# The second q, k, v stage: rows from the matrix engine with the bias in PSUM, turned in fp32, stored in 1 MB pieces

## What is computed

```python
def act_quant(x):                     # per row of 512
    s = 127.0 / clip(max(abs(x)), EPS)
    return clip(round(x * s), -128, 127) / s
def weight_quant(w):                  # -1, 0, 1 times the mean
    s = 1.0 / clip(mean(abs(w)), EPS)
    return clip(round(w * s), -1, 1) / s
def bitlinear(x, w, b):
    return act_quant(x) @ weight_quant(w).T + b
xn  = rmsnorm(x, g1) * (1 + scale) + shift      # scale, shift: one pair of rows per batch
qkv = bitlinear(xn, w_qkv, b_qkv)
q, k, v = split(qkv)                            # attention follows: softmax(q k^T / sqrt(32)) v
```

## Time and profile before

| | |
|---|---|
| median of 3 runs | 4297.87 us (4294.86 to 4299.38) |
| profiled execution | 4297.65 us, its span 4295.9 us, mean granted clock 0.944 |
| busy, share of the span | PE 3864.4 us (90%), DVE 2841.2 (66%), ACT 2651.5 (62%), POOL 850.9 (20%) |
| all DMA | 419.67 MB, mean 98 GB/s |

### The profile page before, as it was taken

One profiled execution on the slowest core, in us unless ns is written; L12 is line 12 of the kernel. 1 busy time (PEld: TensorE's weight loads), 2 busy tenths in 40 slices (PEclk: granted clock), 3 DMA queues, 4 the chain that ended last, 5 costly groups with the idle time before them and its releaser, 6 DMA issues. The chain is left out here.

```text
span 4295.9 us, 69382 instructions
## 1 busy us (share of the span) xinstructions
PE 3864.4 (90%) x26385; PEld 2562.5 (60%) x26436; DVE 2841.2 (66%) x5335; ACT 2651.5 (62%) x4619; POOL 850.9 (20%) x932
## 2 busy tenths in 40 slices
PE   8998999999999554989999945689999999997999
PEld 7875666666666443777788822256666666663444
DVE  3327888888888455333421146678888888886887
ACT  2227888888888222222222224378888888885887
POOL 0015555555555122000000022200000000001221
PEclk9999999999999777999999967789999999998999
DMA  5445332333321455334431044453332223313221
GB/s 184 181 155 130 75 63 58 63 67 71 63 58 28 147 175 175 111 128 140 162 120 49 30 150 176 159 130 62 63 74 63 57 63 67 70 28 128 72 70 42
DMA packets 309208, 419.67 MB, mean 98 GB/s; under 512 B 90959, under 2 KB 167267, under 8 KB 308875
## 3 DMA queue, kind: packets, MB, share of 16 engines
q1 hardware_dynamic: 308878, 415.23, 34.6%
HBM read 257.54 MB, written 157.32 MB: 97 GB/s over the span
## 5 line engine op out<-in xcount | busy, mean ns | idle before, releaser
L555 ACT ACTIVATE Sn<-Sn,mn 128x1024 f32<-128x1024 f32 x1024 | 1175.0, 1147 | 30.6 <-DVE mn L583 18.8
L521 PEld LDWEIGHTS pt<-ident,Sn 128*128 128x128 f32 x8192 | 881.0, 141 | 421.0 <-issue 413.5
L521 PE MATMUL pt<-ident,Sn 128*128 128x128 f32 x8192 | 1123.2, 280 | 1.2 <-DVE PT L547 0.5
L545 ACT ACTIVATE PT<-pt 128x512 f32<-128x512 f32 x1280 | 738.3, 598 | 235.8 <-PE pt L521 235.8
L489 PE MATMUL sp<-KS,QS 97*128 97x512 f32 (+1 forms) x2048 | 733.7, 440 | 40.4 <-DMA KS<-cpad 18.9
L583 DVE CUSTOM_DVE_ANT_0 Sn<-sp,biastile 128x1024 f32<-128x1024 f32 x512 | 624.1, 1219 | 145.2 <-PE sp L489 113.6
L585 DVE TENSOR_SCALAR_CACHE_REDUCE Sn<-sp 128x1024 f32<-128x1024 f32 x512 | 624.0, 1219 | 127.6 <-PE sp L489 127.6
L628 POOL TENSOR_SCALAR biastile<-dist,ascale 128x1024 f32<-128x1024 f32 x512 | 576.0, 1125 | 497.2 <-DVE mn L583 483.5
L510 PE MATMUL po<-PT,Vp 128*32 128x256 f32 x8192 | 651.4, 391 | 0.0
L547 DVE COPY PT<-pt 128x512 f32<-128x512 f32 x768 | 531.0, 691 | 118.9 <-PE pt L521 118.9
L1044 ACT ACTIVATE gf<-pf,b1T 128x512 f32<-128x512 f32 x128 | 88.3, 690 | 562.5 <-PE pf L989 535.9
(11 more groups left out here) (210 smaller groups left out, 4839.9 us busy)
## 6 DMA issues: line engine op xcount, KB each, us to landing
QS<-s_qhi SPq DMA_DIRECT2D x128, 256.0 KB, 5.1
KS<-s_khi SPq DMA_DIRECT2D x128, 256.0 KB, 7.1
KS<-s_klo SPq DMA_DIRECT2D x64, 256.0 KB, 6.1
QS<-s_qlo SPq DMA_DIRECT2D x64, 256.0 KB, 6.9
Vp<-s_v SPq DMA_DIRECT2D x64, 256.0 KB, 7.7
s_o<-og SPq DMA_DIRECT2D x32, 512.0 KB, 8.7
xA<-in_x SPq DMA_DIRECT2D x8, 1024.0 KB, 5.9
s_qhi<-qstage SPq DMA_DIRECT2D x32, 256.0 KB, 2.0
```

What stands on the lines that cost most here:

```text
L521: op = nc.tensor.transpose(ps[:, i, :], sn[:, (g * HALF + i) * P:(g * HALF + i + 1) * P], K.ident[:])
L545: nc.scalar.activation(dst, src, ACT.Copy).then_inc(*s_cp_act.up())
L555: nc.scalar.activation(sn[:], sn[:], ACT.Exp, scale=-1.0, bias=mn[n % 3][:, t:t + 1], accum_out=sums[n % 5][:, t:t + 1]).then_inc(*s_exp.up())
```

## The change

Only stage D changes, and it is the same arithmetic in another order. The quantised tile is the stationary operand for q, k and v alike, so that all three come out as rows (`project`). Each group has a fifth matmul with six rows: six bf16 rows of the bias against six bf16 columns that hold pieces of the inverse scale. So the PSUM tile holds (product + bias / scale), and one multiplication by the scale, a column, ends it: on ACT for q and k (`scale_row`), on DVE for v (`scale_v`). q and k are then turned by PE as fp32 (`turn_row`), and ACT and DVE take the halves out of PSUM (`high_half`, `low_half`; the factor of q is in both). The bias rows are split in three on DVE after the first tile's first operation, and SP places them by three DMAs (`bias_rows`). POOL makes the pieces of the inverse scale (`inverse_pieces`) and the whole inverse root (five small operations, as in stage F); DVE multiplies by G first and by the root with the shift added in one operation. Every engine has a new order. PE works tile by tile, not block by block, in single PSUM tiles (`px`; `pr` for q, k, v; `pT` for q, k). q and k are gathered over four tiles and stored as four DMAs of 1 MB, v as before with four buffers, x with eight. On POOL, iteration s has the scale and the pieces of tile s-2, at each batch's start the product of G, and then the root of tile s.

```diff
+def bias_rows(K, S, name, n, s_raw, s_split, s_row):
+    nc, dve, sp = K.nc, K.dve, K.sp
+    rows, rest = S.sb("brow" + name, [6, n], BF16), S.sb("brest" + name, [6, n])
+    second, third = S.sb("bp2" + name, [6, n], BF16), S.sb("bp3" + name, [6, n], BF16)
+    def load(src):
+        nc.sync.dma_start(rest[:], src.partition_broadcast(6)).then_inc(*s_raw.up(16))
+    def split():
+        dve.wait_ge(s_raw, 16)
+        nc.vector.tensor_copy(rows[:], rest[:]).then_inc(*dve.own.up())
+        dve.settle()
+        nc.vector.tensor_tensor(rest[:], rest[:], rows[:], ALU.subtract).then_inc(*dve.own.up())
+        dve.settle()
+        nc.vector.tensor_copy(second[:], rest[:]).then_inc(*dve.own.up())
+        dve.settle()
+        nc.vector.tensor_tensor(third[:], rest[:], second[:], ALU.subtract).then_inc(*s_split.up())
+    def place():
+        sp.wait_ge(s_split, 1)
+        for row, (_, piece) in enumerate(PIECES):
+            if piece:
+                nc.sync.dma_start(rows[row:row + 1, :], (None, second, third)[piece][row:row + 1, :]).then_inc(*s_row.up(16))
+    return rows, load, split, place
...
+def inverse_pieces(K, rc, left, sc, winv, s_rc):
+    nc, pool = K.nc, K.pool
+    nc.gpsimd.tensor_scalar(left, sc, winv, 1.0, ALU.mult, ALU.mult).then_inc(*pool.own.up())
+    pool.settle()
+    nc.gpsimd.tensor_copy(rc[:, 0:3], left.to_broadcast([P, 3])).then_inc(*pool.own.up())
+    pool.settle()
+    nc.gpsimd.tensor_tensor(left, left, rc[:, 0:1], ALU.subtract).then_inc(*pool.own.up())
+    pool.settle()
+    nc.gpsimd.tensor_copy(rc[:, 3:5], left.to_broadcast([P, 2])).then_inc(*pool.own.up())
+    pool.settle()
+    nc.gpsimd.tensor_tensor(rc[:, 5:6], left, rc[:, 3:4], ALU.subtract).then_inc(*s_rc.up())
...
-        x_l = S.loads("xD", 6, [P, D])
+        x_l = S.loads("xD", 8, [P, D])
...
+        rc, rT = [S.sb(f"rcD{i}", [P, 6], BF16) for i in range(2)], [S.sb(f"rTD{i}", [6, P], BF16) for i in range(2)]
+        sm = [S.sb(f"smD{i}", [P, 16]) for i in range(16)]
+        row = {w: [S.sb(f"{w}rowD{i}", [P, D]) for i in range(2)] for w in "qk"}
+        st = {w: S.stores(w + "stD", 2, [P, 2, DC, BLK], F32R, 2) for w in "qk"}
+        vst = S.stores("vstD", 4, [P, D])
+        px = S.ps("pxD", [P, 2 * D], BF16)
+        pr, pT = {w: S.ps(f"p{w}D", [P, D]) for w in "qkv"}, {w: S.ps(f"pT{w}D", [P, DC, P]) for w in "qk"}
...
+            x, s = x_l.take(sp, i, 1, (s_xg, i + 1), (s_sq, i + 1))
...
-            load_x(0)
             load_b(0)
+            load_bias(a["L1_cond_b_qkv"])
             for i in range(1, 4):
                 load_x(i)
             nc.sync.dma_start(wq[:], K.tern_s["qkv"].rearrange("(c p) n -> p c n", p=P)).then_inc(*s_w.up(16))
+            place_bias()
             for b in range(1, B):
                 load_b(b)
             for s in range(NT + TAIL):
                 if s + 4 < NT:
                     load_x(s + 4)
-                for i, j in groups(s - 1):
-                    if j < 2 * DC:
-                        w, c = "qk"[j // DC], j % DC
-                        buf, sem = qst.of(2 * DC * i + j)
-                        sp.wait_ge(s_qlo, 2 * DC * i + j + 1)
-                        for n, part in enumerate(("hi", "lo")):
-                            nc.sync.dma_start(K.qk_s[w, part][c * P:(c + 1) * P, i * BLK:(i + 1) * BLK],
-                                              buf[:, n, :].bitcast(F32)).then_inc(*sem.up(16))
-                    else:
-                        t = j - 2 * DC
-                        buf, sem = vst.of(TPB * i + t)
-                        sp.wait_ge(s_v, TPB * i + t + 1)
-                        nc.sync.dma_start(K.v_s[i * BLK + t * P:i * BLK + (t + 1) * P, :], buf[:]).then_inc(*sem.up(16))
-            qst.done(sp)
-            vst.done(sp)
-        def turn(i):
-            blk, t = divmod(i, TPB)
-            ps = pt_r.take(pe, i, (s_xT, i + 1))
+                i = s - 4
+                if 0 <= i < NT:
+                    buf, sem = vst.of(i)
+                    sp.wait_ge(s_v, i + 1)
+                    nc.sync.dma_start(K.v_s[i * P:(i + 1) * P, :], buf[:]).then_inc(*sem.up(16))
+                    if i % TPB == TPB - 1:
+                        cols = slice(i // TPB * BLK, (i // TPB + 1) * BLK)
+                        for w in "qk":
+                            buf, sem = st[w].of(i // TPB)
+                            sp.wait_ge(s_lo[w], i + 1)
+                            for n, part in enumerate(("hi", "lo")):
+                                nc.sync.dma_start(K.qk_s[w, part][:, cols].rearrange("(c p) t -> p c t", p=P),
+                                                  buf[:, n].bitcast(F32)).then_inc(*sem.up(16))
+            for r in (vst, st["q"], st["k"]):
+                r.done(sp)
...
+        def turn_x(i):
             pe.wait_ge(s_xq, i + 1)
+            pe.wait_ge(s_rc, i + 1)
+            if i >= 1:
+                pe.wait_ge(s_xT, i)
             for c in range(DC):
...
+                nc.tensor.transpose(px[:, c * P:(c + 1) * P], xq[i % 2][:, c * P:(c + 1) * P], K.identb[:])
+            nc.tensor.transpose(px[0:6, D:D + P], rc[i % 2][:], K.identb[:]).then_inc(*s_Tx.up())
+        def project(i, w):
+            pe.wait_ge(s_xT, i + 1)
+            if i >= 1:
+                pe.wait_ge(s_v if w == "v" else s_e[w], i)
+            cols = slice("qkv".index(w) * D, ("qkv".index(w) + 1) * D)
+            for d in range(DC):
+                nc.tensor.matmul(pr[w][:], xT[i % 2][:, d, :], wq[:, d, cols], start=d == 0, stop=False)
+            nc.tensor.matmul(pr[w][:], rT[i % 2][:], brow[:, cols], start=False, stop=True).then_inc(*s_m[w].up())
+        def turn_row(i, w):
+            pe.wait_ge(s_e[w], i + 1)
+            if i >= 1:
+                pe.wait_ge(s_lo[w], i)
+            for c in range(DC):
+                op = nc.tensor.transpose(pT[w][:, c, :], row[w][i % 2][:, c * P:(c + 1) * P], K.ident[:])
+            op.then_inc(*s_T[w].up())
         def tensor_program():
             pe.wait_ge(s_w, 16)
+            pe.wait_ge(s_row, 48)
             for s in range(NT + TAIL):
...
+                if 0 <= s - 1 < NT:
+                    project(s - 1, "k")
+                    project(s - 1, "v")
+                if s < NT:
+                    turn_x(s)
+                if 0 <= s - 1 < NT:
+                    turn_row(s - 1, "q")
+                    turn_row(s - 1, "k")
+                if s < NT:
+                    project(s, "q")
...
+        def copy_xT(i):
+            act.wait_ge(s_Tx, i + 1)
+            if i >= 2:
+                act.wait_ge(s_m["v"], i - 1)
+            nc.scalar.activation(rT[i % 2][:], px[0:6, D:D + P], ACT.Copy)
+            nc.scalar.activation(xT[i % 2][:], px[:, 0:D].rearrange("p (c q) -> p c q", q=P), ACT.Copy).then_inc(*s_xT.up())
+        def scale_row(i, w):
+            act.wait_ge(s_dq, i + 1)
+            act.wait_ge(s_m[w], i + 1)
+            if i >= 2:
+                act.wait_ge(s_T[w], i - 1)
+            nc.scalar.activation(row[w][i % 2][:], pr[w][:], ACT.Copy, scale=col(i, 9)).then_inc(*s_e[w].up())
+        def high_half(i, w):
+            buf, t = st[w].room(act, i // TPB), i % TPB
+            act.wait_ge(s_T[w], i + 1)
+            nc.scalar.activation(buf[:, 0, :, t * P:(t + 1) * P], pT[w][:], ACT.Copy, scale=factor[w]).then_inc(*s_hi[w].up())
         def scalar_program():
             for s in range(NT + TAIL):
+                if 0 <= s - 5 < NT:
+                    copy_xT(s - 5)
+                if 0 <= s - 6 < NT:
+                    high_half(s - 6, "q")
+                if 0 <= s - 4 < NT:
+                    round_x(s - 4)
+                if 0 <= s - 6 < NT:
+                    high_half(s - 6, "k")
                 if s < NT:
...
+                    square(s)
+                if 0 <= s - 5 < NT:
+                    scale_row(s - 5, "q")
+                    scale_row(s - 5, "k")
...
+        def low_half(i, w):
+            buf, t = st[w].of(i // TPB)[0], i % TPB
+            dve.wait_ge(s_hi[w], i + 1)
+            nc.vector.scalar_tensor_tensor(buf[:, 1, :, t * P:(t + 1) * P], pT[w][:], factor[w], buf[:, 0, :, t * P:(t + 1) * P],
+                                           ALU.mult, ALU.subtract).then_inc(*s_lo[w].up())
...
+        def scale_v(i):
+            buf = vst.room(dve, i)
+            dve.wait_ge(s_dq, i + 1)
+            dve.wait_ge(s_m["v"], i + 1)
+            nc.vector.tensor_scalar(buf[:], pr["v"][:], col(i, 9), 1.0, ALU.mult, ALU.mult).then_inc(*s_v.up())
...
+        def vector_program():
+            nc.vector.reciprocal(winv[:], K.wmean[:, 0:1]).then_inc(*s_winv.up())
+            for s in range(NT + TAIL):
+                if s < NT:
+                    times_g(s)
+                if 0 <= s - 1 < NT:
+                    normalise(s - 1)
+                if 0 <= s - 2 < NT:
+                    quantise(s - 2)
+                if 0 <= s - 4 < NT:
+                    low_half(s - 4, "q")
```

(72 more changed lines are left out.)

170 lines of the change are left out of this document (34 added, 136 removed).

## The result

The changed kernel takes 4204.85 us, median of four runs (4201.7 to 4206.9); the kernel before took 4298.62 beside it (4294.86 to 4299.98, four runs). The ratio is 0.9785, 95% interval 0.9773 to 0.9796. The forecast was 4209 us, range 4182 to 4256.

What follows compares the result with a forecast made beforehand. Stage D was taken as bound by a ring of waits through the engines, no engine full. Head 27, 31 x 5.2, cold clock 6, bursts 7 and tail 18.5 sum to 219.7 against 308.5 us, so 4209 us; range 4182 to 4256.

Steps and rivals of the forecast that it cites:

- head: Stage D's start to the first projection, set by ACT's square(4) waiting for its x load: 27 us.
- 31 steps: Stage D's tiles after the first, PE the longest engine, at 5.2 us each.
- cold clock: PE at 1.2 GHz at the stage's start, for a tile and a half at 3.9 us extra: 6 us.
- bursts: x loads queued on SP behind 4.2 MB of q, k stores: 1 us for each of 7 blocks, 7 us.
- tail: After the last q projection: remaining work, last 4.2 MB of stores, landing and barrier, 18.5 us.
- the ring: Old stage D: each tile passes ACT, DVE, POOL, DVE, PE, ACT in turn, 9.6 us a tile with no engine full.
- the wait on ACT's copy: PE must not project before ACT copies turned x: about 0.95 us, of which row turns cover only 0.85.
- The end value of 1.38 a group: PE's matmul group if the bias row costs as in fp32r; 1.2 us was taken.
- Nor does it delay anyone: POOL, at 4.0 us a tile, has its pieces ready as the tile is quantised, one iteration later.
- Even: 0 at best: ACT's wait for x behind each store burst: 0 at best, 3 us a block at worst, 1 taken.
- neither clock one: Rivals on PE's clock: stays at 1.2 GHz, 4322 us, 6 in 100; swings at 0.71, 4255 us, 9 in 100.
- the second's premise: Swinging-clock rival: part of PE's work, suspects 13 transposes a tile, does not count for the clock; 9 in 100.

Runs made afterwards that it cites:

- breaking the ring alone: Kernel before with DVE's quantised tile written first, ACT's square one tile earlier and four v store buffers, old arithmetic kept: 4218.64 us, ratio 0.9816.
- the padded kernel: Changed kernel with the bias matmul on 128 rows instead of six, 122 of them zero: 4184.98 us, ratio 0.9744.
- At 4.49 a tile: Changed kernel with 128-row bias, tile 4's x loaded earlier, bias split first, G product two tiles ahead, last block stored in halves: 4172.91 us, ratio 0.9714.
- the run where the clock rose later: Changed kernel with POOL's product with G for the next batch made four tiles ahead of its use: 4208.57 us, one run.

## Why the prediction was right

**The sum by its terms**, predicted and measured (us):

| term | predicted | measured |
|---|---|---|
| head | 27 | 28.2 |
| 31 steps | 31 x 5.2 = 161.2 | 31 x 5.25 = 162.8 |
| cold clock | 6 | 2.7 (7.98 - 5.25) |
| bursts | 7 | 0 |
| batch starts | not in the sum | 3.2 (three steps of 6.30) |
| tail | 18.5 | 17.9 |
| stage | 219.7 | 214.9 |

**What bounds before.** Confirmed: breaking the ring alone is worth 81 of 93.6 us.

**The tile on PE.** The 5.2 was right by two errors that cancel. PE's work was put at 4.75, and it is 5.25: the group is 1.28, not 1.2 (0.24 in all), the bf16 turns 0.48, not 0.32, the row turns 0.93, not 0.85. With the padded tiles these are 1.08, 0.28 and 0.05 less for the row turns, so nearly all of it comes from the tiles of six rows and six columns. The forecast saw that the bias row starts 0.10 late in the earlier trace rows but not that the group after it starts late as well. The 0.45 for the wait on ACT's copy (0.3 of it for the first matmul after a wait, which stood on no row) didn't exist: ACT's copy ends at 2611.02, within the 0.93 of row turns and 0.09 before q's projection, and the timeline has no idle time there. That the time a tile is nearly the forecast one is luck. The wait is real at a shorter tile, 0.08 us in the padded kernel. The end value of 1.38 a group had been kept in the range, and the truth lay between.

**DVE, ACT, POOL.** By their windows at 5.25 a tile they are busy for 4.5, 4.0 and 3.6 us. For DVE 4.5 was forecast and for ACT 4.4. POOL's 4.0 was not busy time but the time from first to last, pauses between its operations with it, and that is 4.47 by the run without bias rows. The scaled row on ACT, for which no row had the form, took 0.67 and 0.69 (0.67 taken). So POOL is no bound at 5.25, as said, but nearer to one than was said, and the bound once PE needs less. Of its 1-wide operations, counted at about 0.37 each, some took far more: 0.56 for the power, up to 0.96 for the first of the pieces. "Nor does it delay anyone" was wrong: its product with G stands ahead of a root and holds DVE at each batch's start, 3.2 us. From the waits of the changed kernel (total us, times, longest), ACT's for x and DVE's for the product:

```profile
ACT sqD L1334 <- DMA xD<-s_x: 35.3, 3, 21.9
...
DVE xnD L1383 <- POOL Gada L1208: 17.5, 4, 8.6
```

**Transfers.** "Even: 0 at best" was the value that came: ACT's three waits for x all lie in the head. DMA has a share of 0.77 at 285 GB/s (0.85 and 302 forecast). The load behind a burst is issued 3.8 us after its begin (2579.22 against 2575.46), as SP needs that long for the four issues, and not 1 us; but it lands 13.1 to 14.2 us after the begin, where 13 to 14 were forecast. What was off is when ACT needs it: 15.1 or 16.1 us after the begin and not 14, so there were 0.9 to 3.0 us to spare. At 4.49 a tile the need comes first, after 12.7 to 12.9 us, and the term comes back: ACT waits 1.7 to 2.0 us a block, and the step grows by 1.3 to 1.7.

**The head.** The mechanism was right to the wait: SP's row DMAs come 15.0 us after the stage's start (16.7 forecast), ACT's square(4) is idle for 8.4 us for the load, the projection is 28.2 in. The split of the bias was faster than forecast and the load later: square(4) starts 26.8 in, and 25.1 was forecast, as the six issues ahead of the load take SP 3.0 us (2516.12 to 2519.12). Loading that tile first takes 5.1 us off.

**The tail.** 17.9 against 18.5, again by two errors: the q stores begin 5.9 us after the last q projection (2702.13), not 4.3, and from there to the next stage it is 12.0 us and not 14.2, in part because the bytes move at 381 GB/s and not 345.

**The clock.** It is at 1.2 GHz for the first q and k projections (bias rows of 0.60 us at 2529.28 and 2531.63) and at the upper level by the end of the first v (0.39 at 2533.72). The second tile is at full speed, as forecast. The cold start was put at a tile and a half and cost 0.7 of one, 2.7 us and not 6; in the run where the clock rose later it was 4.3 and 1.2, so the 6 was within what can come. Of the rivals, neither clock one occurred, and doubling the transposes speaks against the second's premise. (Its 6.9 us a tile is a little high: 4.75 over 0.71 is 6.7. It changes nothing.)

**The total.** 4209 against 4204.85. The stage was forecast 4.8 us too long, which is what was put too high (cold clock, bursts and tail, 10.9) less what was too low or left out (batch starts, steps and head, 6.0). The mechanisms held but for two, the wait for ACT's copy and POOL's product; that the sum is so near is in part luck.

## What to carry to other kernels

Before new arithmetic, look for the ring: one tile's timeline showed it, and moving two operations (with two more store buffers) gave 86% of the gain. A small matmul in a row of full ones costs more than its columns: pad it to 128 rows and columns if its bytes are free, and look whether the weight load lies ahead of its matmul. An engine whose small operations depend on each other can be the limit at a busy share of 85% (3.78 of 4.47 us): count the pauses, and look who waits for it. The time from issue to landing says little when the issue itself moves: count from the start of the burst. When one engine becomes the limit, gains at the head, the tail and in the step add only until the transfers are full; work out the bytes over the best measured rate first.

## What the runs showed of the hardware

A bf16 matmul with six rows between full ones costs 0.42 us instead of 0.22 (0.20 more each), its weight load starting 0.01 us ahead instead of 0.22; a stationary tile of six columns among transposes costs the same 0.20, and 0.05 more at the turn behind it. Sizes between 6 and 128 were not tried. With 16 fp32 transposes and 5 bf16 ones a tile, 2.28 of 6.13 us, the granted clock was 1.00. Stores of 256 KB and of 1 MB gave nearly the same stage (213.0 and 214.9, 188.4 and 187.5), and at 5.25 us a tile a load behind 4.2 MB of them landed 13.8 to 14.6 and 13.1 to 14.2 us after the burst's first issue. Eleven small operations of POOL, each after the one before, took 4.47 us with 3.78 busy. All 16 DMA engines together reached 381 GB/s at a share of 0.98.
